# A graph network on one core: dense layers by groups of tiles, one reading of the weighted sum, and one-hots shared out differently in the building

## The reference, cut to what matters

```python
h = relu(layernorm(x))                       # before each layer
x = x + attention(h, qW, kW, vW)             # layer 0, softmax over each node's edges

def sage(x, Wp, bp, Ws, Wn, b):
    m = relu(x @ Wp + bp)
    agg = segment_max(m[src], dst)           # 0 where a node has no edge
    return x @ Ws + agg @ Wn + b
h = l2norm(relu(sage(h, Wp1, bp1, Ws1, Wn1, b1)))
h = l2norm(sage(h, Wp2, bp2, Ws2, Wn2, b2))
x = x + h                                    # layer 1

support = h @ weight_G                       # layer 2
x = x + segment_sum(support[dst] * edge_weight[:, None], src) + bias_G

deg = 1 + in_degree                          # layer 3: K = 16 steps, ALPHA = 0.1
h = x0 = relu(layernorm(x))
for _ in range(16):
    h = 0.9 * segment_sum(norm * h[row], col) + 0.1 * x0    # with self loops
x = x + h
```

## Time and profile before

| | |
|---|---|
| time, median of 3 runs | 2891.17 us (2879.86 to 2897.45) |
| the profiled execution's own time | 2871.62 us |
| its span | 2869.9 us, 70218 instructions |
| TensorE busy | 2447.4 us (85%) |
| VectorE busy | 1805.2 us (63%) |
| ScalarE busy | 1187.8 us (41%) |
| GpSimd busy | 1128.0 us (39%) |
| DMA | 227.27 MB, mean 79 GB/s |

### The profile page before, as it was taken

The page is one execution under the profiler, slowest core; times in us unless marked ns, Lnnn a source line. Parts: engine busy times, 40 slices in busy tenths (PEclk is TensorE's granted clock), DMA queues, the critical chain, the costliest instruction groups (busy, mean ns, idle before and its releaser), DMA issues. The chain is left out here.

```text
span 2869.9 us, 70218 instructions
## 1 busy us (share of the span) xinstructions
PE 2447.4 (85%) x27871; PEld 1951.2 (68%) x27871; DVE 1805.2 (63%) x5324; ACT 1187.8 (41%) x2826; POOL 1128.0 (39%) x1407
## 2 busy tenths in 40 slices
PE   6778999985888888666888888368799999999999
PEld 4445777763555665434656655258699999999998
DVE  6997999986677777535877777241244444444444
ACT  5997888874434444422444444231221111111110
POOL 4005999983666666436666666310000000000000
PEclk7557999996898999877999999569999999999999
DMA  5103000003454555523555545539400000000000
GB/s 161 41 2 98 13 12 13 12 27 110 123 135 125 128 140 136 135 75 85 143 132 135 142 124 144 164 108 328 141 2 2 2 2 2 2 2 2 2 2 18
DMA packets 156204, 227.27 MB, mean 79 GB/s; under 512 B 59488, under 2 KB 121659, under 8 KB 155202
## 3 DMA queue, kind: packets, MB, share of 16 engines
q1 hardware_dynamic: 129390, 184.69, 21.5%
q0 software_dynamic: 22944, 36.72, 6.5%
q10 hardware_dynamic: 3540, 1.30, 0.2%
HBM read 122.26 MB, written 100.35 MB: 78 GB/s over the span
## 5 line engine op out<-in xcount | busy, mean ns | idle before, releaser
L1886 POOL DMA_INDIRECT max_row<-table,max_src_rows x640 | 664.5, 1038 | 445.0 <-issue 163.2
L2490 PE MATMUL prop<-g,adj 128*128 128x192 f16 x9216 | 770.6, 246 | 7.1 <-PEq L2161 7.1
L2490 PEld LDWEIGHTS prop<-g,adj 128*128 128x128 f16 x9216 | 759.5, 98 | 14.9 <-issue 12.4
L1913 PE MATMUL max_far<-adj 128*96 128x512 f16 x1800 | 543.7, 404 | 14.0 <-issue 12.0
L1758 POOL TENSOR_SCALAR e<-e 128x512 f32<-128x512 f32 (+1 forms) x625 | 365.8, 604 | 198.6 <-ACT e L1746 180.9
L2035 DVE TENSOR_SCALAR adj<-adj,node_numbers 128x512 f16<-128x512 f16 x900 | 306.2, 352 | 200.0 <-PE max_far L1913 120.7
L1772 DVE TENSOR_TENSOR e<-e,a_ps 128x1024 f32<-128x1024 f32 (+1 forms) x313 | 372.2, 1194 | 32.9 <-PE a_ps L1684 13.2
L2579 ACT ACTIVATE g<-prop_state 128x96 f16<-128x96 f32 (+1 forms) x375 | 106.0, 283 | 635.0 <-DVE prop_state L2547 635.0
L1746 ACT ACTIVATE e<-s_ps 128x512 f32<-128x512 f32 (+1 forms) x625 | 335.5, 585 | 60.3 <-PE o_ps L1696 38.5
L2545 DVE SCALAR_TENSOR_TENSOR part<-prop,coef,prop_base 128x96 f32<-128x96 f32 x384 | 120.5, 314 | 313.0 <-PE prop L2490 226.2
L1913 PEld LDWEIGHTS max_far<-adj 128*96 128x96 f16 x1800 | 214.4, 136 | 93.9 <-issue 29.1
(11 more groups left out here) (280 smaller groups left out, 3352.6 us busy)
## 6 DMA issues: line engine op xcount, KB each, us to landing
weights<-max_rows_w SPq DMA_DIRECT2D x52, 400.0 KB
rows_dram<-max_out SPq DMA_DIRECT2D x100, 192.0 KB
weights<-adj SPq DMA_DIRECT2D x48, 400.0 KB
ws_w<-weights SPq DMA_DIRECT2D x50, 384.0 KB
max_same<-same_dram SPq DMA_DIRECT2D x196, 96.0 KB
rows_dram<-adj SPq DMA_DIRECT2D x96, 192.0 KB
ws_w<-weights SPq DMA_DIRECT2D x50, 288.0 KB
max_row<-table,max_src_rows POOLq DMA_INDIRECT x640
```

The source lines that it names most:

```text
L1886: nc.gpsimd.indirect_dma_start(row[i % RING][:, j, :], None, table_dram, bass.IndirectOffsetOnAxis(ap=src_rows[:, 4 * n + j:4 * n + j + 1] ...
L1913: mm = nc.tensor.matmul(far_ps[j % 2][0:D, :], parts[:, k, a, :], hot[(T * j + k) % HOTS], start=k == a == 0, stop=k == T - 1 and a == 1)
L2490: return nc.tensor.matmul(sums(step, t), adj[:, k, t * P:(t + 1) * P], states[:, k, :], start=start and t % 2 == 0, stop=k == END - 1 and ...
```

## The change

Four parts.

**Building.** VectorE makes the lanes of all windows of a step (`own` is 0 for lanes). ScalarE makes the first *key* one-hot of every even step, by Abs and Relu over 125 keys, so it helps in two steps of four, not three.

**second_layer.** The 25 single tiles become seven groups (`DENSE`, 4, 4, 4, 4, 4, 3 and 2 tiles); each engine's instruction that can take a group does so (PSUM copies, adds, splits, roots), and a step has group s in its first half and group s-1 in its second. Two times three `fill`s stand in a step in place of one per tile. `multiply(g)` writes one `out_ps` of two banks and waits for `lo_kept` and `own_kept` of the group before. The rectification and the first split are one ScalarE instruction.

**third_layer.** The same, over three lags (s, s-1, s-2). The additions go in place into `own`.

**sum_and_propagate** takes the place of `weighted_layer` and `propagate`, with no block boundary between them. The matrix is read once, in 100 units of half rows (1600 columns, 3200 bytes a row, 409.6 KB a unit) through 6 slots; the sums of 25 target tiles lie in five banks, five tiles of 96 columns each, and the high and the low part are two matmuls into the same columns. The half row cuts tile 12 in two, so a unit has 2 x 13 matmuls of 96 columns. All the work behind the sums comes after the last unit, in five groups of five tiles. In step 0 of the propagation TensorE waits for `first_low` at every fifth k. `base` and `g1` of the propagation lie in the slots' memory, its small buffers in that of `support_parts`.

The diff, cut to its core:

```diff
+DENSE = ((0, 4), (4, 4), (8, 4), (12, 4), (16, 4), (20, 3), (23, 2))
...
+            def turn_agg(g):
+                t, m = DENSE[g]
+                pe.wait_ge(picked[g], 16 * m)
+                if g >= 2:
+                    pe.wait_ge(agg_copied, g - 1)
+                for i in range(m):
+                    mm = nc.tensor.transpose(agg_ps[g % 2][0:D, i * P:(i + 1) * P], agg[:, t + i, :], c.ident[:, :])
...
+            def multiply(g):
+                pe.wait_ge(o_copied, g + 1)
+                if g >= 1:
+                    pe.wait_ge(lo_kept, g)
+                    pe.wait_ge(own_kept, g)
+                for i in range(DENSE[g][1]):
+                    mm = nc.tensor.matmul(out_ps[:, i, 0:2 * D], oT[:, g % 2, i * P:(i + 1) * P], w[:, :], start=True, stop=True)
+                mm.then_inc(multiplied, 1)
...
-            for s in range(LAST_STEP):
-                if s == MULTIPLY:
+            for s in range(G + 1):
+                if s == 1:
                     pe.wait_ge(w_loaded, 64)
                     pe.wait_ge(ones_made, 1)
-                if s >= MULTIPLY:
-                    multiply(s - MULTIPLY)
-                if 0 <= s - TURN_O < T:
-                    turn_o(s - TURN_O)
-                if 0 <= s - 1 < T:
-                    sum_agg(s - 1)
-                if s < T:
+                if s < G:
                     turn_agg(s)
-                fill(nc, c, adj, fill_ps, 1)
+                    fill(nc, c, adj, fill_ps, STEP_FILL)
+                    sum_agg(s)
+                if s >= 1:
+                    turn_o(s - 1)
+                    fill(nc, c, adj, fill_ps, STEP_FILL)
+                    multiply(s - 1)
...
-            for s in range(LAST_STEP):
-                if s >= MULTIPLY:
-                    pool_rows(s - MULTIPLY)
-
-                if s > MULTIPLY and group_of[s - 1 - MULTIPLY] < group_of[s - MULTIPLY]:
-                    keep_high(group_of[s - 1 - MULTIPLY])
-                if 0 <= s - TURN_O < T:
-                    copy_o(s - TURN_O)
-                if s - 1 in pair_ending:
-                    root(pair_ending[s - 1])
-                if s < T:
+                nc.scalar.activation(parts[:, tiles(g), 0, :], out_ps[:, 0:DENSE[g][1], 0:D], ACT.Relu).then_inc(hi_kept, 1)
+
+            def keep_own(g):
+                act.wait_ge(multiplied, g + 1)
+                if g >= 2:
+                    act.wait_ge(stored[g % 2], 16 * (g // 2))
+                nc.scalar.activation(kept[:, g % 2, 0:DENSE[g][1], :], out_ps[:, 0:DENSE[g][1], D:2 * D], ACT.Copy).then_inc(own_kept, 1)
+
+            for s in range(G + 1):
+                if s < G:
                     copy_agg(s)
-            keep_high(len(GROUPS) - 1)
+                if s >= 1:
+                    copy_o(s - 1)
+                if s < G:
+                    root(s)
+                if s >= 1:
+                    keep_own(s - 1)
+                    keep_high(s - 1)
...
+            for s in range(G + 1):
+                if s < G:
+                    add(s)
+                    normalise(s)
+                if s >= 1:
+                    keep_low(s - 1)
...
-            for s in range(LAST_STEP):
-                if s == MULTIPLY:
+            for s in range(G + 2):
+                if s < G:
+                    turn_agg(s)
+                if s == 2:
                     pe.wait_ge(wg_loaded, 16)
-                if 0 <= s - MULTIPLY < T:
-                    multiply(s - MULTIPLY)
-                if 0 <= s - TURN_H < T:
-                    turn_h(s - TURN_H)
-                if 0 <= s - 1 < T:
-                    sum_agg(s - 1)
-                if s < T:
-                    turn_agg(s)
+                if s >= 2:
+                    multiply(s - 2)
+                if s < G:
+                    sum_agg(s)
+                if 1 <= s <= G:
+                    turn_h(s - 1)
...
-            for s in range(LAST_STEP + 1):
-                if 0 <= s - MULTIPLY < T:
-                    keep_high(s - MULTIPLY)
-                if 0 <= s - TURN_H < T:
-                    copy_h(s - TURN_H)
-                if s - 1 in pair_ending:
-                    root(pair_ending[s - 1])
-                if s - 2 in pair_ending:
-                    root_variance(pair_ending[s - 2])
-                if s < T:
+            for s in range(G + 2):
+                if 1 <= s <= G:
+                    root_variance(s - 1)
+                if s < G:
                     copy_agg(s)
-                if s - 2 in pair_ending:
-                    normalise(pair_ending[s - 2])
+                if s >= 2:
+                    keep_high(s - 2)
+                if 1 <= s <= G:
+                    normalise(s - 1)
+                if s < G:
+                    root(s)
+                if 1 <= s <= G:
+                    copy_h(s - 1)
...
-            for s in range(LAST_STEP + 1):
-
-                if 0 <= s - 1 - MULTIPLY < T:
-                    keep_low(s - 1 - MULTIPLY)
-                if 0 <= s - 1 < T:
-                    add(s - 1)
-                if s - 1 in pair_ending:
-                    grow(pair_ending[s - 1])
-                if s - 2 in pair_ending:
-                    scale_up(pair_ending[s - 2])
+            for s in range(G + 2):
+                if s < G:
+                    add(s)
+                if 1 <= s <= G:
+                    scale_up(s - 1)
+                if s < G:
+                    square_up(s)
+                if s >= 2:
+                    keep_low(s - 2)
+                if s < G:
+                    grow(s)
...
-        helped = [g for g in range(STEPS_USED) if g % QUARTER < QUARTER - 1]
+        helped = [g for g in range(STEPS_USED) if g % 2 == 0]
+        helps_until = lambda g: (g + 1) // 2
...
-                nc.vector.tensor_tensor(lane_hot[:, g % RINGS, own:n, :].rearrange("p w (n a) -> p w n a", a=2),
-                                        c.iota16[:, 0:P].rearrange("p (n a) -> p n a", a=2).unsqueeze(1).to_broadcast([P, n - own, P // 2, 2]),
-                                        lanes_of[q][:, first + own:first + n, :].unsqueeze(2).to_broadcast([P, n - own, P // 2, 2]), ALU.is_equal).then_inc(lanes_ready, 1)
-                for w in range(n):
+                nc.vector.tensor_tensor(lane_hot[:, g % RINGS, 0:n, :].rearrange("p w (n a) -> p w n a", a=2),
+                                        c.iota16[:, 0:P].rearrange("p (n a) -> p n a", a=2).unsqueeze(1).to_broadcast([P, n, P // 2, 2]),
+                                        lanes_of[q][:, first:first + n, :].unsqueeze(2).to_broadcast([P, n, P // 2, 2]), ALU.is_equal).then_inc(lanes_ready, 1)
+                for w in range(own, n):
                     s = first_win[g] + w
...
-                    pe.wait_ge(hot_ready, first_win[g] + w + 1)
+                    if w == 0 and g in helped:
+                        pe.wait_ge(first_key_made, helped.index(g) + 1)
+                    else:
+                        pe.wait_ge(hot_ready, first_win[g] + w + 1 - helps_until(g + 1))
...
+            def first_key(g):
                 act.wait_ge(distance_made, helped.index(g) + 1)
-                nc.scalar.activation(lane_hot[:, g % RINGS, 0, :], distance[:, helped.index(g) % 2, :], ACT.Relu, scale=-1.0, bias=c.ones[:, 0:1]).then_inc(lane_made, 1)
-
-            for g in range(RINGS - 1):
...
-        units = [(n, k, h) for n in range(len(PASSES)) for k in range(T) for h in range(2)]
...
-                sp.dma_start(w[u % SLOTS][:, 0:m], weights_dram[k, h, :, :, first[n] * P:first[n] * P + m].rearrange("a d n -> (a d) n")).then_inc(loaded[u % SLOTS], 16)
...
-                for j in range(PASSES[n]):
...
-                    mm = nc.tensor.matmul(sums(t), w[u % SLOTS][:, j * P:(j + 1) * P], parts[:, k, :, :].rearrange("p r d -> p (r d)"),
-                                          start=k == h == 0 and j % 2 == 0, stop=last, skip_group_check=True)
...
+    SLOTS, COLUMNS = 6, NP // 2
...
+        late = sb("weights_then_states", [P, SLOTS, COLUMNS], F16)
+        w = [late[:, i, :] for i in range(SLOTS)]
+        after = late[:, :, :].rearrange("p s n -> p (s n)")
+        base = after[:, 0:2 * T * D].bitcast(F32).rearrange("p (t d) -> p t d", d=D)
...
+        units = [(k, h, s) for k in range(T) for h in range(2) for s in range(2)]
...
+        def weighted(t):
+            return ps[BANKS - WEIGHED + t // FIVE][:, t % FIVE * D:(t % FIVE + 1) * D]
...
+            for u, (k, h, s) in enumerate(units):
+                pe.wait_ge(loaded[u % SLOTS], 16 * (u // SLOTS + 1))
+                first, last = k == h == 0, k == T - 1 and h == 1
+                for t in range(COLUMNS * s // P, -(-COLUMNS * (s + 1) // P)):
+                    begin, end = max(t * P, COLUMNS * s), min((t + 1) * P, COLUMNS * (s + 1))
+                    rows = slice(begin - t * P, end - t * P)
+                    for r in range(2):
```

(94 more changed lines are left out.)

609 lines of the change are left out of this document (238 added, 371 removed).

## The result

The median falls from 2887.65 to 2853.25 us (nine runs of each), a ratio of 0.9882 with a 95% interval of 0.986 to 0.9904: 34 us less, in the range, but 22 us short of the forecast difference of 56. The execution profiled with this result took 3438.18 us at a mean granted clock of 0.636, which no other run of either kernel did (the ratio leaves it out), so "after" is the profile of E5, the changed kernel run again.

What follows compares the result with a forecast made beforehand. No engine bounds the whole: propagation TensorE, building ScalarE, weighted layer DMA, dense layers chains of waits. Terms -18 - 17 - 6 - 19.5 + 4.3 = -56.2 us take the execution from 2871.6 to 2815.4, the median to 2835; range 2805 to 2868.

Steps and rivals of the forecast that it cites:

- Building: Building of the matrix: the period of four steps falls from 3.31 to some 2.94 us, -18 us.
- gets nothing new: Building: TensorE, busy 2.4 us of a period, gets no new work.
- Second layer: second_layer by groups: ends at 1275, -17 us (-9 to -22).
- The step of 5.3 us: second_layer: a group of four takes TensorE 4 x 1.32 = 5.3 us.
- so I have 12 tiles (three groups) summed by 1252: second_layer, window of gathers: fewer hand-offs let 12 tiles be summed by 1252, where 7 were.
- rival 1: Both layers: groups gain nothing while gathers run; second layer -4, third +4, 23 us less gained, 2858; chance 0.22.
- Third layer: third_layer by groups: one ring through four engines, 8.0 us a group, -6 us (-13 to +3).
- The last two groups (3 and 2 tiles) drain in two steps: End of third_layer: the short groups drain in two steps, within the term of -6 us.
- Reading: Weighted sum: half-row loads at 358 GB/s take 114.4 us, last sums at 2031.5, -19.5 us (-15 to -21).
- just hidden: Weighted sum: matmuls of 96 columns at 42 ns, 1.09 us a unit, stay below the DMA's 1.14 us.
- The rule of the Trainium skill: Weighted sum: about 81 ns for 128 columns, so 2600 matmuls near 200 us as an estimate, median near 2920.
- Behind the sums: Last sums to the end of step 0's first part: 21.6 us where 17.3 were, +4.3 us (+1 to +7).

Runs made afterwards that it cites:

- E5: The changed kernel itself, run again in the sittings of the experiments: 2670.19 us against 2698.33 for the kernel before, ratio 0.9885.
- E12: E7 with the last four units of the reading in another order: 2849.12 us against 2886.77 for the kernel before, ratio 0.9867.
- E8: The changed kernel without the low part's matmuls in the weighted sum (1300 in place of 2600): the sum took 114.6 us.
- E9: The changed kernel with loads of only 128 of 1600 columns from the seventh unit on, all 2600 matmuls kept: the sum took 120.8 us.
- E6: The kernel before, unchanged, profiled again beside the experiments: span 2695.0 us, second layer 52.8, third 66.9.
- E7: The changed kernel with the third layer of before (single tiles): 2667.39 us, ratio 0.9886 to the kernel before; third layer 66.9 us.

## Why the prediction was right or wrong

**Building, right.** -18 forecast, -19.6 measured, with VectorE as the new bound (2.91 us a period, 2.94 forecast). That TensorE "gets nothing new" did not hold for its busy time (2.8 us a period, not 2.4), but it did not come to bind.

**Second layer, mechanism half right.** The step of 5.3 us held (additions 16.0, 21.2, 26.5 and 31.8 us into the layer in E5). What failed is the step "so I have 12 tiles (three groups) summed by 1252". In the sitting with late hand-offs only group 0, four tiles, was summed when the last gather had been issued (E12): a group needs fewer hand-offs, but each is as late as the next and they stand in series. The start was misread too: the addition of 1251.26 is that of the fifth tile, not the 7th, in the trace of before; TensorE turned the seventh at 1254.22, but only five were summed by 1252. The gain was 6.5 us there, from one profile of each kind. In the other sittings it was 4.5 in the mean (52.7 to 54.9 us by tiles in four profiles, 47.9 to 51.7 by groups in seven), of a forecast 17. That is rival 1. Its price (-4) was near.

**Third layer, ring right, count wrong.** 8.0 us a group were forecast and 8.15 measured, in part by luck: VectorE's work is 4.6 us, not 5.3, and its waits are 3.5 us, not 2.7. "The last two groups (3 and 2 tiles) drain in two steps" is the failed step: I counted the gain in tiles, but the layer pays by groups, 7.6 and 7.1 us for the last two, and the first addition waits for four gathers. +3.8 to +4.7 in place of -6, all in sittings without late hand-offs. For the kind of sitting of the prediction there is only the execution profiled with the result, in which this layer had a granted clock of 0.50 as in all the others: 84.8 us, against 84.4 (before) and 84.0 (E12) by tiles. So for that kind a loss of 4 us is not shown, and no gain either.

**Reading, mis-sized.** The DMA's 114.4 us were right (114.6 alone, E8). The term that failed is the 42 ns a matmul, "just hidden": it is 44.7 (E9), just above the 44 at which it stops being hidden. 42 stood on no row (half of the 81 ns of 192 columns would be 40.5). 2600 x 44.7 ns are 116.2 us by themselves; the start at half clock, for which the forecast had no term, adds 2 to 5 (a wait of 1.16 us for a load in E5 is in it), and the loads beside the matmuls 1 to 4. With them it is 121.0 to 124.7 us where 114.4 were forecast: -8.6 in E5 instead of -19.5. The rule of the Trainium skill cited ahead (page "TensorE: Matmul & The Clock Gate", section "Back-to-back issue gap") has about 81 ns for 128 columns in a stream of fresh weights. This case does not bear it out: 96 columns took 44.7 ns (447 in 20.00 us, E9), and 192 columns, more than the page's 128, took 81 ns.

**Behind the sums, right in kind, too dear.** +4.3 forecast, 17.8 to 19.5 us measured, +1.7 (the kernel before took 16.5 to 17.8 in its five profiles): VectorE begins 1.8 us ahead of the sums' end (bank 0 is done early), and its additions stand 2.2, 2.7, 3.3 and 3.2 us apart, not 3.3 each.

**Sum.** Three steps were too kind, the second layer by 13 us, the third by 10 and the reading by 11; building and the end gave 4 back. 56 became 26 in E5 against E6. The 34 of the result fit this, as an estimate: the second layer gains 6.5 there instead of 3.6, and the third, by its one profile, loses 0.4 instead of 3.9, which makes 32 to 33. That is the number of rival 1 (33), but with another make-up: the reading gained 11 less than there, the third layer lost less, and building and the end gave some back. The forecast difference was missed by two fifths; the range held because it reached to rival 1, not because the terms were right.

## What to carry to other kernels

Count a grouped stage in rings, not in tiles: a short last group costs nearly a full one, and the first starts later. In the third layer grouping took work off VectorE and not off the ring, so it gained next to nothing a tile (8.15 us for four against 2 x 4.14 in E7). Where a transfer and an engine are forecast within a few per cent of each other, give both limits the range that their rows leave, and add what the start costs at a low clock: here it was 114.6 us for the one alone, 120.8 for the other, 121.0 to 124.7 together. Where VectorE and ScalarE were both nearly full, swapping which of them makes what still gained 12% of the period, and the period counted instruction by instruction from starts in the trace came out within 2%. Profile the kernel before more than once before a stage of waits is priced: the same code took 76.8 or 52.8 us.

## What the runs showed of the hardware

- While GpSimd issues indirect gathers, hand-offs between the other engines can come up to 13.5 us late, all at once (E12), or not at all (E5, E6), with the same code: second layer of the kernel before 76.8 or 52.8 us, third 84.4 or 66.9, passes of maxima 1061 or 928 us in all (1079 in E12). It was one or the other for a whole sitting. What sets it was not found. The sittings were on different chips, none twice, so whether it belongs to the chip or to the sitting is open.
- A stream of 96-column matmuls, each with new weights, runs at 44.7 ns a matmul (447 in 20.00 us at clock 1.00, E9).
- Rows of 3200 bytes out of a matrix read in halves: 351 to 382 GB/s (E8), as fast as whole rows of 3072 bytes.
